# Macaron attention's output product for two units at once, in three float32r passes

## The reference, cut to what matters

```python
qkv = h @ wqkv                          # h: x with half its features shifted by a token
q, k = l2norm(q) * qs, l2norm(k) * ksc  # 8 heads of 64
q, k = rotary_xpos(q, k)
o = local_attention(q, k, v)            # windows of 64, each looks one back
x = x + o @ wo                          # wo: 512 x 128, the product that is changed
h = shift_token(x)
h = (h - mu) / sqrt(var + 1e-5) * lg + lb
a, g = split(h @ w1 + b1)
x = x + (a * gelu(g)) @ w2 + b2
```

## Time and profile before

| | us |
|---|---|
| median of three runs (2122.40 to 2123.63) | 2122.96 |
| profiled execution | 2117.76 |
| its span, first to last instruction | 2115.9 |
| TensorE busy in it | 1819.0 (86%) |
| VectorE busy | 1571.3 (74%) |
| ScalarE busy | 1398.0 (66%) |
| GpSimd busy | 1284.5 (61%) |
| one item in the middle of a phase, from one centring (L1610) to the next | 38.7 to 38.8 |
| output products (L1600), 1024 instructions | 137.0 busy |

### The profile page before, as it was taken

How to read it: one execution, slowest core, us unless ns; L and a number is a source line. 1 busy time by engine, 2 the same in 40 slices (tenths; PEclk the granted TensorE clock), 3 DMA queues, 4 the chain that set the end, 5 groups by cost and what they waited for, 6 DMA issues and landing times. The chain is left out here.

```text
span 2115.9 us, 51807 instructions
## 1 busy us (share of the span) xinstructions
PE 1819.0 (86%) x16844; PEld 1388.3 (66%) x16845; DVE 1571.3 (74%) x2828; ACT 1398.0 (66%) x3956; POOL 1284.5 (61%) x1099
## 2 busy tenths in 40 slices
PE   4499776289955999999999997766999999999996
PEld 3488623278833777777777774334777777777773
DVE  6788767778855888788788883335888787888882
ACT  5555441345544888888878874555878888888783
POOL 3674300666415888878788872005888788787870
PEclk9999888589967999999999998788999999999998
DMA  6332310133151111111110110000110111111101
GB/s 210 86 91 57 84 54 1 56 97 87 39 149 44 27 29 22 25 24 27 24 28 21 22 29 1 4 0 18 27 29 20 27 24 27 24 26 22 25 22 40
DMA packets 87308, 88.26 MB, mean 42 GB/s; under 512 B 13978, under 2 KB 65863, under 8 KB 87016
## 3 DMA queue, kind: packets, MB, share of 16 engines
q1 hardware_dynamic: 77288, 68.09, 12.9%
q0 software_dynamic: 8704, 17.85, 2.5%
q10 hardware_dynamic: 1152, 0.25, 0.1%
HBM read 35.60 MB, written 22.22 MB: 27 GB/s over the span
## 5 line engine op out<-in xcount | busy, mean ns | idle before, releaser
L2058 POOL TENSOR_TENSOR mac_probs<-mac_probs,mac_prec 128x512 f32<-128x512 f32 x256 | 265.0, 1041 | 194.3 <-DVE mac_prec L1873 193.8
L1734 ACT ACTIVATE mac_probs<-banks,mac_nmax 128x128 f32<-128x128 f32 x1024 | 358.7, 385 | 0.0
L1830 DVE TENSOR_TENSOR route_pool<-banks,tables 128x1024 f32<-128x1024 f32 x256 | 300.6, 1214 | 33.7 <-ACT route_pool L1694 28.3
L2038 POOL TENSOR_TENSOR route_pool<-route_pool 128x1024 f32<-128x1024 f32 x128 | 303.3, 2369 | 35.7 <-issue 13.1
L1864 DVE TENSOR_REDUCE mac_nmax<-banks 128x4 f32<-128x512 f32 x256 | 164.8, 685 | 125.0 <-PE banks L1562 125.0
L2049 POOL TENSOR_TENSOR mac_qkn<-route_pool,mac_rc 128x1024 f32<-128x1024 f32 x128 | 243.6, 1903 | 16.4 <-issue 7.3
L876 POOL DMA_INDIRECT x_sorted<-route_pool,route_index x128 | 125.7, 982 | 185.8 <-DVE route_index L680 102.8
L1734 ACT ACTIVATION_READ_ACCUMULATOR mac_probs<-banks,mac_nmax 128x1 f32 x1024 | 231.9, 226 | 0.0
L884 POOL DMA_INDIRECT y_tokens<-moe_bench,moe_goal x144 | 140.7, 977 | 118.1 <-DVE moe_bench L827 77.9
L54 PE MATMUL banks<-wqkv_h,mac_hh 128*128 128x512 f32 x384 | 179.5, 467 | 27.0 <-POOL mac_hl L2013 22.1
L1744 ACT ACTIVATE mac_pts<-banks 128x512 f32<-128x512 f32 x256 | 147.2, 596 | 43.1 <-PE banks L1573 40.4
(11 more groups left out here) (321 smaller groups left out, 5015.3 us busy)
## 6 DMA issues: line engine op xcount, KB each, us to landing
mac_v_even<-mac_v SPq DMA_DIRECT2D x224, 128.0 KB, 2.2
moe_xs<-x_sorted SPq DMA_DIRECT2D x144, 72.0 KB
route_pool<-y_tokens SPq DMA_DIRECT2D x16, 512.0 KB, 7.2
y_tokens<-moe_bench,moe_goal POOLq DMA_INDIRECT x144, 2.3
moe_bench<-in_L_attn_x SPq DMA_DIRECT2D x8, 256.0 KB, 6.0
route_pool<-in_L_ffn_W SPq DMA_DIRECT2D x4, 512.0 KB, 7.0
b<-in_b_flat SPq DMA_DIRECT2D x1, 2048.0 KB, 10.8
x_sorted<-route_pool,route_index POOLq DMA_INDIRECT x128, 2.3
```

The source lines that it names most:

```text
L1734: e = act.activation(probs[:, r, p, :], m.ps[:, S + r, p * P:(p + 1) * P], ACT.Exp, bias=nmax[:, r, p:p + 1], accum_out=psum[:, r, p:p + 1])
L1830: turn = dve.tensor_tensor(turned[:, i, :, :].rearrange("q k (h s j) -> q k h s j", s=2, j=DH // 2), q[:, :, :, ::-1, :] if i else q, tabl ...
L2038: pool.tensor_tensor(sums[:], turned[:, 0, :, :], turned[:, 1, :, :], ALU.add).then_inc(added, 1)
L2058: pool.tensor_tensor(probs[:, r, :, :], probs[:, r, :, :], prec[:, r, :].unsqueeze(2).to_broadcast([P, HP, P]), ALU.mult).then_inc(shared[ ...
```

## The change

- The weights `wo` are loaded into a buffer of the setup phase. ScalarE copies them into a float32r part and VectorE subtracts to get the rest (two instructions each).
- `keep_out` (VectorE, each unit) now writes the attention output of a unit into one half of a float32r buffer `oh` for two units, waits for that, and subtracts to write the rest into `ol`.
- `output` multiplies two units at once: four products by three float32r passes of 256 columns. The product of units 0 and 1 is at the front of unit 3, before the projection of keys, and `values` comes after that projection there. The product of units 2 and 3 is at the end of unit 0 of the next item, where the product of unit 3 was.
- `add_out` adds 256 columns, twice an item: in unit 3 behind `reciprocals(n, 1)`, in unit 0 where it was.
- `values` for units 1 and 3 waits for `ol_kept` of the unit before; for units 0 and 2 it waits for `u_done` of the pair before.
- To find room, `fr` shares its buffer with `fq` and `fn` with the first third of `gate`, and three buffers of the mixture phases move into their own scope.

```diff
@@ -1309,7 +1309,7 @@
...
         w.h, w.l = sb(f"wqkv_h{l}", [P, 3, T], F32R), sb(f"wqkv_l{l}", [P, 3, T], F32R)
-        w.wo = sb(f"wo{l}", [P, HP, P])
+        w.woh, w.wol = sb(f"wo_h{l}", [P, HP, P], F32R), sb(f"wo_l{l}", [P, HP, P], F32R)
         w.w1h, w.w1l = sb(f"w1_h{l}", [P, 2 * HID], F32R), sb(f"w1_l{l}", [P, 2 * HID], F32R)
@@ -1326,11 +1326,11 @@
...
         raws, raw1s = sb("raw_qkv", [P, 2, 3 * T]), sb("raw_gated_w1", [P, 2, 2 * HID])
-        raw_masks = sb("raw_masks", [P, 2, T])
+        raw_masks, raw_wos = sb("raw_masks", [P, 2, T]), sb("raw_wo", [P, 2, HP, P])
         scales, lnw, b1 = sb("qk_scales", [P, 2, 4, DH]), sb("ln_w", [P, 2, 2]), sb("b1_raw", [P, 2, 2 * MC])
...
         rest_in, rest2_in, extras_in = sem("rest_in"), sem("rest2_in"), sem("extras_in")
-        biased, steps, cleared = sem("biased"), [sem(f"steps{l}") for l in range(2)], sem("cleared")
+        biased, steps, cleared, wo_hi = sem("biased"), [sem(f"steps{l}") for l in range(2)], sem("cleared"), sem("wo_hi")
         block = c.block()
@@ -1346,7 +1346,7 @@
...
             for l, w in enumerate(ws):
-                sp.dma_start(w.wo[:], ins["L1_ffn_wo"][l].rearrange("(j p) d -> p j d", p=P)).then_inc(rest_in, 16)
+                sp.dma_start(raw_wos[:, l, :, :], ins["L1_ffn_wo"][l].rearrange("(j p) d -> p j d", p=P)).then_inc(rest_in, 16)
                 sp.dma_start(w.w2[:MW, 0:2, :], ins["L1_ffn_w2"][l][0:2 * MW, :].rearrange("(j p) d -> p j d", p=MW)).then_inc(rest_in, 16)
@@ -1409,6 +1409,9 @@
...
             dve.tensor_scalar(raw1, raw1, lnw[:, 0, 0:1], None, ALU.mult).then_inc(steps[0], 1)
+            for l in range(2):
+                dve.wait_ge(wo_hi, START + l + 1)
+                dve.tensor_tensor(ws[l].wol[:], raw_wos[:, l, :, :], ws[l].woh[:], ALU.subtract)
             dve.wait_ge(steps[0], done + 2)
@@ -1442,6 +1445,10 @@
...
                     lns[b % WAYS].scale(act, b // WAYS)
+            act.wait_ge(rest_in, START + REST)
+            for l, w in enumerate(ws):
+                act.activation(w.woh[:].rearrange("p j d -> p (j d)"), raw_wos[:, l, :, :].rearrange("p j d -> p (j d)"),
+                               ACT.Copy).then_inc(wo_hi, 1)
 
@@ -1470,10 +1477,13 @@
...
         psum, prec = sb("psum", [P, H2, HP]), sb("prec", [P, H2, HP])
-        pts, ot = sb("pts", [P, H2, T]), sb("ot", [P, HP, P])
-        fs, fq, fr, fn = sb("fs", [P, T]), sb("fq", [P, T]), sb("fr", [P, T]), sb("fn", [P, T])
+        pts = sb("pts", [P, H2, T])
+        oh, ol = sb("oh", [P, HP, H2 * P], F32R), sb("ol", [P, HP, H2 * P], F32R)
+        fs, fq = sb("fs", [P, T]), sb("fq", [P, T])
+        fr = fq
         fh, fl = sb("fh", [P, T], F32R), sb("fl", [P, T], F32R)
         gate = sb("gate", [P, MC, T])
+        fn = gate[:, 0, :]
         prod = spare[:, 8 * T:(8 + MC) * T].rearrange("q (i t) -> q i t", i=MC)
@@ -1485,7 +1495,8 @@
...
         pt_done, pt_kept = [sem(f"pt_done{r}") for r in range(H2)], [sem(f"pt_kept{r}") for r in range(H2)]
-        pv_done, ot_kept, y_done, u_done, v_kept = sem("pv_done"), sem("ot_kept"), sem("y_done"), sem("u_done"), sem("v_kept")
+        pv_done, oh_kept, ol_kept, y_done, u_done, v_kept = (
+            sem("pv_done"), sem("oh_kept"), sem("ol_kept"), sem("y_done"), sem("u_done"), sem("v_kept"))
         v_copied = [sem(f"v_copied{t}") for t in range(NT)]
@@ -1579,7 +1590,10 @@
...
                 pe.wait_ge(v_copied[t], START + V_MOVES[t] * (j + 1))
-                pe.wait_ge(u_done, START + k)
+                if t % 2:
+                    pe.wait_ge(ol_kept, START + k)
+                else:
+                    pe.wait_ge(u_done, START + 2 * j + t // 2)
                 for r in range(H2):
@@ -1590,14 +1604,15 @@
...
 
-            def output(k, j, lay):
-
-                if not live(k):
-                    return
-                wo = ws[layer(j, lay)].wo
-                pe.wait_ge(ot_kept, START + k + 1)
+            def output(j, s, lay):
+
+                if not there(j):
+                    return
+                w = ws[layer(j, lay)]
+                pe.wait_ge(ol_kept, START + NT * j + 2 * (s + 1))
                 for p in range(HP):
-                    mm = pe.matmul(m.ps[:, O, :P], wo[:, p, :], ot[:, p, :], start=(p == 0), stop=(p == HP - 1))
+                    mm = mm3(pe, m.ps[:, O, :H2 * P], (w.woh[:, p, :], w.wol[:, p, :]), (oh[:, p, :], ol[:, p, :]),
+                             start=(p == 0), stop=(p == HP - 1))
                 mm.then_inc(y_done, 1)
@@ -1651,8 +1666,13 @@
...
                         down(i - 2, lay)
-                    values(n - 1, *before)
-                    project(n + 3, *ahead, lay, 1)
+                    if t == 3:
+                        output(i, 0, lay)
+                        project(n + 3, *ahead, lay, 1)
+                        values(n - 1, *before)
+                    else:
+                        values(n - 1, *before)
+                        project(n + 3, *ahead, lay, 1)
                     if t == 1:
@@ -1665,7 +1685,8 @@
...
                     turn_probs(n, 0)
-                    output(n - 1, before[0], lay)
+                    if t == 0:
+                        output(i - 1, 1, lay)
                     if t == 2:
@@ -1872,21 +1893,26 @@
...
 
-            def keep_out(k):
+            def keep_out(k, j, t):
 
...
                 dve.wait_ge(pv_done, PV_BASE + k + 1)
-                dve.wait_ge(y_done, START + k)
-                dve.tensor_copy(ot[:].rearrange("q p k -> q (p k)"), m.ps[:, O, :]).then_inc(ot_kept, 1)
-
-            def add_out(k, j, t, lay):
-
-                if not live(k):
-                    return
-                cols = bass.ds(start_of(j, lay) + t * P, P)
-                dve.wait_ge(y_done, START + k + 1)
-                dve.tensor_tensor(m.u[:, cols], m.ps[:, O, :P], m.u[:, cols], ALU.add).then_inc(u_done, 1)
+                if t % 2 == 0:
+                    dve.wait_ge(y_done, START + 2 * j + t // 2)
+                half = slice(t % 2 * P, (t % 2 + 1) * P)
+                dve.tensor_copy(oh[:, :, half], m.ps[:, O, :].rearrange("q (p k) -> q p k", k=P)).then_inc(oh_kept, 1)
+                dve.wait_ge(oh_kept, START + k + 1)
+                dve.tensor_tensor(ol[:, :, half], m.ps[:, O, :].rearrange("q (p k) -> q p k", k=P), oh[:, :, half],
+                                  ALU.subtract).then_inc(ol_kept, 1)
+
+            def add_out(j, s, lay):
+
+                if not there(j):
+                    return
+                cols = bass.ds(start_of(j, lay) + s * H2 * P, H2 * P)
+                dve.wait_ge(y_done, START + 2 * j + s + 1)
+                dve.tensor_tensor(m.u[:, cols], m.ps[:, O, :H2 * P], m.u[:, cols], ALU.add).then_inc(u_done, 1)
 
@@ -1947,15 +1973,17 @@
...
                     if t == 3:
+                        add_out(i, 0, lay)
                         product(i - 1, lay, 0)
...
                         f_add(i - 2, lay)
-                    keep_out(n - 1)
+                    keep_out(n - 1, *before)
                     clip(n + 2)
                     rotate(n + 3, *ahead, lay)
-                    add_out(n - 1, *before, lay)
+                    if t == 0:
+                        add_out(i - 1, 1, lay)
                     maxima(n + 1, 1)
@@ -2024,7 +2052,7 @@
...
                     return
-                pool.wait_ge(u_done, START + NT * (j + 1))
+                pool.wait_ge(u_done, START + 2 * (j + 1))
                 pool.wait_ge(f_centred, START + j)
@@ -2310,15 +2338,16 @@
...
         m.base0, m.steps = sb("base0", [P, HALVES, NE]), sb("steps", [P, CAP // P + LATE])
-        m.low_bf, m.ones_bf = sb("low_bf", [P, P], BF16), sb("ones_bf", [P, P], BF16)
         m.order = sb("order", [P, NE])
-        m.blank, m.ids = sb("blank", [P, WIDE]), sb("ids", [P, PAIRS // P + 1])
+        m.ids = sb("ids", [P, PAIRS // P + 1])
         x_sorted = nc.dram_tensor("x_sorted", [ROWS, WIDE], F32)
...
         with ExitStack() as moe:
+            m.low_bf, m.ones_bf = [moe.enter_context(nc.sbuf_tensor(n, [P, P], BF16)) for n in ("low_bf", "ones_bf")]
+            m.blank = moe.enter_context(nc.sbuf_tensor("blank", [P, WIDE], F32))
             w = moe_weights(nc, moe)
```

## The result

The change makes the kernel slower: 2185.2 us (median of four runs, 2184.2 to 2188.1) against 2122.7 us (four runs, 2121.9 to 2123.6), a ratio of 1.0297 with the interval 1.0279 to 1.0315. That is 62.5 us more. The forecast of 2208 us had the direction, and its range held the time; its 85 us were 23 us too many.

A forecast was written before the change was run, and what follows sets the result against it. Waits for ScalarE's copies and VectorE's rotation, not TensorE's load, were taken as the bound. Units' 2.0 + 0.65 + 0.1 + 0 = 2.75 us an item, times 31, gave +85 us: 2208 us, range 2155 to 2225.

The forecast's parts named there:

- The product's price: TensorE's new output product: twelve float32r passes of 256 columns at 0.116 us, 1.48 us in all.
- Unit 3, +2.0: Product at the front delays values, which wait 0.4 us for VectorE's addition to u; L1533 comes 2.0 us later.
- two equal chains: Unit 3, values to next L1533: VectorE's rotation gives 1025.76, TensorE with ScalarE's copy 1025.58, against 1023.73 before.
- VectorE's 0.8 us: Converting copy, wait and subtraction in place of the copy alone: 0.8 us more VectorE work in each unit.
- +0.65 by the rotation: Unit 0: VectorE's later rotation delays L1533 by 0.70 us, TensorE's chain by 0.49; with a little given back, +0.65.
- Unit 1, +0.1: Gain of 0.04 us from the product leaving, met by some 0.1 us delay through GpSimd's copies: +0.1 us.
- Unit 2, 0: ScalarE's copy of v still decides and the rotation has room, so the unit's time does not change.
- The count of 31: Of 32 items in the two phases, 31 were counted as full ones, giving +85 us.
- The setup, 0: Weight-part subtractions on VectorE, 1.4 us, fit in the 2.2 us before GpSimd's end, so they cost nothing.
- TensorE as the bound: Rival: stalls hidden, each item 1.0 us shorter, 31 us in all, 2092 us; chance 0.09.
- the middle case: Rival: units 3 and 0 stall, units 1 and 2 give back 0.98 us each; 2147 us, chance 0.13.
- Only the work: Rival: units 3 and 0 add only product work, 1.97 us an item, 2184 us; lower end of the 0.72-chance forecast.

The follow-up runs named there:

- e1: Kernel before with one of the four output products of each unit instead of four: 2110.7 us, ratio 0.9948.
- e5: Kernel after with unit 3's addition to u moved ahead of VectorE's sum of squares and reciprocals: 2229.1 us, ratio 1.0229 to the kernel before.
- e6: Kernel after without VectorE's subtraction and the wait before it, the product taking the rounded part twice: 2244.0 us, ratio 1.0293 to the kernel before.
- e11: Kernel after with one of the three passes of the product at the end of unit 0: 2184.7 us, ratio 1.0296 to the kernel before.
- e9: Kernel before with ScalarE's GELU table load in unit 2 behind the copies of turned probabilities and v: 2115.1 us, ratio 0.9964.
- e10: Kernel after with the later GELU table load of e9: 2189.3 us, ratio 1.0319 to the kernel before.
- e7: Kernel after with the first pair's product behind unit 2's second gated part, its addition behind unit 2's rotation: 2197.0 us, ratio 1.0084 to the kernel before.
- e8: e7 with the second turn of the probabilities before the variance and second gated part in units 1 and 3: 2193.7 us, ratio 1.0068 to the kernel before.
- e12: e4 with the clip as a minimum of two tensors, one constant, instead of tensor and number: 2202.7 us, ratio 1.0083 to the kernel before.
- e4: Kernel before plus VectorE's wait and subtraction behind each output copy, the float32 product waiting for it: 2141.8 us, ratio 1.0097.

## Why the prediction was right, and where its sizes were off

**What bounds the kernel: right.** TensorE's 97% was no bound. With less work it took longer, and e1 shows that the end of a unit hides the product. The scores start 0.10 us after ScalarE's copy, for which 0.15 was taken, and in unit 2 the idle time for the copy of v grew from 0.24 to 1.13 us, close to the 1.2 forecast.

**The product's price: right.** 1.50 us in unit 3 and 1.57 in unit 0, for 1.48 forecast; 0.117 us a pass, for 0.116.

**Unit 3, +2.0: right, +1.93.** The first gated part comes 1.94 us later behind the start of turning q and k: 2.91 before (that L1533 starts at 1014.78; the gated part at 1017.69), 4.85 after (992.53 to 997.38); 1.89 was forecast. The idle time before the values was 0.55 for 0.4, ended by the addition, as e5 shows by its 0.50. Which of two equal chains ends it was open, at 2.03 and 1.85. It is the one over TensorE and ScalarE's copy; e6 removes the subtraction and the unit stays. VectorE's chain was the wrong one of the two because of the next point.

**VectorE's 0.8 us: the step that failed.** Its work was sized well: 0.66, 0.69 and a wait of 0.04 between the end of the one and the start of the other, so that the clip behind them starts 0.73 us later in unit 3 and 0.70 in unit 0. But it was added to a chain in which one member, the clip of 0.64 us in unit 0 and 0.75 in unit 3, was taken for work. It was a wait for GpSimd, and it shrinks when it starts later. Of 0.8 us 0.14 remained in unit 3 and 0.48 in unit 0. So the rotation does not hold unit 0, and its +0.65 by the rotation became +0.52 by TensorE, the chain that the prediction had at 0.49: the product's 0.59 (1.57 for 0.98), less 0.07 for an earlier start. By e11 the rotation alone would have held it at 8.45, which is +0.28: the 0.48 less a margin of 0.20, since the hand-off from the rotation takes 0.05 us and not the 0.15 that was taken for it. The idle time ahead of L1533 that was named as a sign did not appear. Between the copy and the rotation of the earlier trace rows lies the clip of 0.75 us for 16 elements; it was among the rows that I left out, and it should have raised the question.

**Unit 1, +0.1: off by its sign.** It was -0.06: the gain of 0.04 for the product that left stands in full, and the delay by GpSimd did not come. e11 shows that the chain over GpSimd is there, but it is bound to the addition in unit 0, whose lateness the longer unit 0 already holds.

**Unit 2, 0: right.** 12.47 in both. e9 and e10 show that the idle time in it is not worth what it measures.

**The count of 31: wrong.** The first phase grew by 31.2 us and the second by 34.2, together 65.4, which is 27.4 items of 2.39. From centring to centring, the first 14 intervals of a phase, 28 in all, are longer by 2.36 us each in the mean (32.5 us in the first phase, 33.6 in the second), and the stretch ahead of the first centring by 1.4 and 1.5. The rest falls short: the last interval changes by -1.27 and +0.31 us, and the time from the last centring to the end of the phase by -1.46 and -1.19. In that last stretch the same matmuls run at another clock. The windows that begin with the last centring of the first phase, before and then after, with the columns of the earlier trace rows:

```profile
1299.00:1302.00 3.00, 2.07 (x2) 0.50 (x2) 0.00 (x0) 0.26 (x1) 0.57 (x1) 0.55 0.00 0
```

```profile
1333.00:1335.50 2.50, 1.31 (x3) 0.48 (x4) 0.00 (x0) 0.60 (x1) 0.45 (x1) 0.83 0.00 0
```

The clock granted is 0.55 of full speed before, so mostly the level of 1.2 GHz, and 0.83 after, mostly that of 2.4. In both kernels TensorE had idled 1.7 to 1.9 us just ahead of it; ahead of that stood one product of 1.16 us, now one of 1.69. From the centring to the variance it is 2.77 us before and 1.81 after, which is 0.96 of the 1.46. The last interval of the first phase holds such a stretch before too: the passes of its gated parts are 0.43 us apart, for 0.23 elsewhere, behind a wait of 1.72. The merged product is not shown to be the cause. In e10, which has it, the same step from centring to variance takes 2.76 us at a granted clock of 0.50 in the first phase and 1.81 at 1.00 in the second, and e9, which has one unit's product there, shows the same pair. So about 1 us a phase of what falls short is the level that this execution happened to have, and the intervals that grow in full are 28 and not 31.

**The setup, 0: wrong by 1.2 us.** The timeline of GpSimd before, and that of GpSimd and VectorE after:

```profile
650.12 2.27 POOL L1370 TENSOR_SCALAR last_raw_gated_w<-last_raw_gated_w,last_ln_w 128x682 f32<-128x682 f32 x1
```

```profile
650.16 2.86 POOL L1370 TENSOR_SCALAR last_raw_gated_w<-last_raw_gated_w,last_ln_w 128x682 f32<-128x682 f32 x1
...
654.08 1.89 POOL L109 TENSOR_TENSOR w_l<-last_raw_gated_w,w_h 128x682 fp32r<-128x682 f32 x1
...
650.54 1.84 DVE L1414 TENSOR_TENSOR wo_l<-last_raw_wo,wo_h 128x512 fp32r<-128x512 f32 x2
```

The sum asked whether VectorE's added work fits ahead of GpSimd's end. It just does, though the two subtractions take 0.92 us each and not 0.69: VectorE ends at 654.72, where GpSimd ended at 654.69. But GpSimd's own instructions are longer: the multiplication (L1370) takes 2.86 us for 2.27 beside the new subtractions, and its last subtraction 1.89 for 1.39, since VectorE, which had been done by 652.48, now works until 654.72. GpSimd's end is the later one, and the first phase begins 1.2 us later. Both VectorE subtractions there have two SBUF inputs, unlike those that read a bank. That this is the cause is argued from the trace; no run tried it.

**The sum.** 85 us forecast, 62.5 measured: 11 for the terms of an item (0.36 x 31), 9 for the count (3.6 x 2.39), less 1 for the setup, and 4 because the profiled execution of before lay 5 us below its median and that of after 1 below.

**The rivals.** TensorE as the bound (2092) and the middle case (2147, units 1 and 2 giving back) are refuted by e1 and by the table of units. "Only the work" (2184) has the right time by another way: it takes 1.97 us an item for all 31, with VectorE catching up; in truth an item costs 2.39 and the count is lower. That it came out within 2 us of the measured time is chance. Its thought that VectorE catches up was the better half of it.

## What to carry to other kernels

Before you count an engine's work as time, find the wait that its next consumer ends on: here three quarters of a product could go for 12 us (e1), while moving one product ahead of a queue cost 44 (e7). Behind each wait that you remove look for the second that stands less than its length behind it; e10 and e11 each took a hold away and gave all of the gain to the next one, and e8 kept it in one unit of two. And ask of each short instruction in a chain whether its time is work: a length far above that of the same instruction elsewhere, as 0.64 for 0.17 us here, points to a wait, and the wait gives way when work is put ahead of it.

## What the runs showed of the hardware

- The clip, a VectorE instruction of 16 elements with all its operands in SBUF, takes 0.17 us beside an idle GpSimd and up to 1.03 beside a running one, and ends 0.02 to 0.10 us behind it, with one source (41 of 41 before) as with two (25 of 25 in e12). A reciprocal of 4 elements, one source in SBUF, takes 0.16 to 0.18 us either way. In the other direction a GpSimd multiplication took 2.86 us for 2.27 beside VectorE subtractions with two SBUF inputs.
- A float32r pass of 256 columns with its weight load repeats every 0.117 us. An eight-instruction float32 product over 128 columns takes 0.98 us, so merging two of them into twelve passes saved 0.4 us of TensorE for two units (1.57 for 1.96).
- From the end of ScalarE's copy to the matmul that it releases it was 0.10 us, from the end of VectorE's rotation 0.05 (996.51 to 996.56 in e4), and from that of its addition 0.22.
